# Score stacks gathered by sixteen rows a DMA, eight apart, from terms laid out pair by pair in DRAM

## The chip, the cores and the metric

The kernel runs on one core of a Trainium2 chip. The metric is the device time of one execution in microseconds (us). The core has a matrix engine (TensorE, PE in the rows), a vector engine (VectorE, DVE), a scalar engine (ScalarE, ACT), GpSimd (POOL), and a sync engine (SyncE, SP), and 16 DMA engines that move data between DRAM and the on-chip memory of 128 partitions. In this kernel SP issues nearly all DMAs; a row of "SPq" is SP issuing them.

## The reference

Four small transformer blocks are applied one after another to an activation of 4 sequences x 512 tokens x 128 features. The first two concern us: block 0 is a cross-attention, block 1 a causal self-attention, a cross-attention and a mixture of experts. All of them have 16 heads of 8 features and take exact fp32 products. Cut to the part that the change touches:

```python
q = (target @ wq).reshape(b, tq, 16, 8)
k = (context @ wk).reshape(b, tk, 16, 8)
v = (context @ wv).reshape(b, tk, 16, 8)
scores = jnp.einsum('bqhd,bkhd->bhqk', q, k) * (1.0 / np.sqrt(8))
...
attn = jax.nn.softmax(scores, axis=-1)
out = jnp.einsum('bhqk,bkhd->bqhd', attn, v).reshape(b, tq, d)
```

The context has 154 tokens; in the causal self-attention keys and queries are the same 512 tokens.

## The kernel before

The work is cut into units, one for each sequence of each stage. Units 0 to 3 are the cross-attention of block 0 (stage L0), 4 to 7 the self-attention (SELF), 8 to 11 the cross-attention of block 1 (CROSS). These 12 "exact" units run from the start to about 590 us. Then come the experts (MOE), two quantised attentions, a feed-forward, a grouped attention and another feed-forward, which the change leaves alone.

**The stacks.** A head has only 8 features, and the score product has to be as exact as fp32. So q and k are each split into three bf16 terms, and eight products of terms are summed (`Q_TERMS`, `K_TERMS`: 0·0, 0·1, 1·0, 0·2, 2·0, 1·1, 1·2, 2·1). The eight products are laid under one another along the contraction: 8 products x 8 features = 64 rows (`STACK`) for one head, and two heads make a pair and fill 128 partitions. There are eight pairs. The stack of queries (`q_stack`) is thus [128 partitions, 8 pairs, 512 tokens] in bf16, 1 MB, the stack of keys is `k_stack` (1 MB, units 4 to 7) or `k_stack_ctx` (8 pairs x 160 columns, 320 KB, cross units). Each has two buffers, for even and odd units. A score matmul (L1106, L1110 in cross units, L1115 in self units) takes the 64 rows of one half as a whole, so the order of the rows within a half does not matter, if it is the same for q and k.

**How a stack is made.** VectorE (L1665 to L1667) leaves the three terms in `parts` with the 128 features on the partitions. They go through DRAM: SP writes each term with one DMA (L818, three for k and three for q), waits until they have landed (`k_out`, `q_out`), and reads them back into the stack. For one unit SP does, in order: write k's terms, write q's terms, read the keys (L800), wait for q's terms, read the queries (L807). Self units' first keys are read ahead of q's writes. In unit 0 ScalarE's queue reads the keys (L1493), and SP reads the queries in two lots: two pairs, then six. Behind the queries of unit 0, unit 5 and unit 9 other loads stand in SP's queue: feed-forward weights (L836), the clearing of `by_expert` (L840), and the experts' weights (L844 to L848).

**What waits for it.** TensorE's order is written out by slots. The parts of unit u+1 are made in the first slots of unit u, and the first scores of unit u+1 are placed three slots ahead of the end of unit u (`AHEAD = 3`). At the first score of a unit TensorE waits for the whole stack of keys and of queries. TensorE's queue is in order, so everything behind that matmul waits as well. VectorE takes the row maxima of each score (L1960), ScalarE the exponentials (L1509), TensorE the transposed scores (L1137, L1149, L1155) and the weighted sums (L1175, L1177).

The lines that do it:

```python
if i == 0:
    pe.wait_ge(k_stacked, 32 * len(K_TERMS) * (u + 1))
    if u:
        pe.wait_ge(q_stacked, 32 * len(Q_TERMS) * (u + 1))
```

Of the kernel before, what the change touches and what calls it, by code (L numbers as in the profile page):

```python
# [6 lines left out]
B, TOKENS, CTX, D = 4, 512, 154, 128  # L7
P = 128
# [40 lines left out]

Q_TERMS = [0, 0, 1, 0, 2, 1, 1, 2]  # L50
K_TERMS = [0, 1, 0, 2, 0, 1, 2, 1]
STACK = len(Q_TERMS) * HD

# [342 lines left out]
def build(nc, io, out):  # L396
# [3 lines left out]
    with ctx:  # L400
# [83 lines left out]
        def place(area, at):  # L484

            def put(shape, dt=fp32):
# [8 lines left out]
                if len(shape) == 2:  # L495
# [86 lines left out]
        up_bank = [score[0][:, 0, :], score[0][:, 1, :], score[1][:, 0, :], score[1][:, 1, :]]  # L582


        scratch = {side: nc.dram_tensor(f"{side}_terms", [2 * HD, 3, PAIRS, TOKENS], bf16)
                   for side in "qk"}

        k_terms_ctx = nc.dram_tensor("k_terms_ctx", [2 * HD, 3, PAIRS, P + 32], bf16)

        by_expert = [nc.dram_tensor(f"by_expert{g}", [EXPERT_BLOCKS * P, D], fp32) for g in range(2)]  # L590
        from_expert = [nc.dram_tensor(f"from_expert{g}", [EXPERT_BLOCKS * P, D], fp32) for g in range(2)]
# [191 lines left out]
        with nc.Block() as block:  # L783

            @block.sync
            def _(sp):
                for u in EXACT_UNITS:
                    width = P + 32 if is_cross(u) else TOKENS
                    keys = (k_stack_ctx if is_cross(u) else k_stack)[:, u % 2, :, :]
                    k_terms_of = (k_terms_ctx if is_cross(u) else scratch["k"]).ap()  # L790

                    def read_keys():
                        sp.wait_ge(k_out, 48 * (u + 1))
                        if u >= 2 and u != SELF * B:

                            sp.wait_ge(scoresT_ready, FIRST_SLOT[u - 1])
                        for s in range(2):
                            for n, term in enumerate(K_TERMS):
                                r = slice(s * STACK + n * HD, s * STACK + (n + 1) * HD)
                                sp.dma_start(keys[r, :, :], k_terms_of[s * HD:(s + 1) * HD, term, :, :])\  # L800
                                    .then_inc(k_stacked, 16)

                    def read_queries(pairs, stacked):
                        for s in range(2):
                            for n, term in enumerate(Q_TERMS):
                                r = slice(s * STACK + n * HD, s * STACK + (n + 1) * HD)
                                sp.dma_start(q_stack[r, u % 2, pairs, :], scratch["q"].ap()[s * HD:(s + 1) * HD, term, pairs, :])\  # L807
                                    .then_inc(stacked, 16)

                    for side in "kq":  # L810
                        wide, terms_of = (width, k_terms_of) if side == "k" else (TOKENS, scratch["q"].ap())
                        terms, done, stacked = (K_TERMS, k_out, k_stacked) if side == "k" else (Q_TERMS, q_out, q_stacked)
                        sp.wait_ge(parts_ready, 2 * u + (1 if side == "k" else 2))
                        if u:
                            sp.wait_ge(stacked, 16 * 2 * len(terms) * u)

                        for t in range(3):
                            sp.dma_start(terms_of[:, t, :, :].rearrange("r c k -> c r k"), parts[side][:, t, 0:wide])\  # L818
                                .then_inc(done, 16)
                        if u == SELF * B and side == "k":  # L820

                            read_keys()
                    if u and u != SELF * B:
                        read_keys()
                    sp.wait_ge(q_out, 48 * (u + 1))
                    if u >= 2:

                        sp.wait_ge(scoresT_ready, FIRST_SLOT[u - 1])
                    if u == 0:

                        read_queries(slice(0, 2), q_first)
                    read_queries(slice(0 if u else 2, PAIRS), q_stacked)
                    if u == 0:
                        for dst, src in [(e_b2[:, :], io["L1_xattn_e_b2"]), (ff_w1[:, :], io["L2_xattn_ff_w1"]),
                                         (ff_w2[:, :, :], io["L2_xattn_ff_w2"].rearrange("(c p) d -> p c d", p=P))]:
                            sp.dma_start(dst, src).then_inc(ff_in, 16)  # L836
                    if u == 5:

                        for g in range(2):
# [89 lines left out]
            def _(pe):  # L929
# [152 lines left out]
                def scores_exact(u, i):  # L1082

                    c, n = exact_steps(u)[i]
                    at_step = STEP_BASE[u] + i
                    if i == 0:
                        pe.wait_ge(k_stacked, 32 * len(K_TERMS) * (u + 1))
                        if u:
                            pe.wait_ge(q_stacked, 32 * len(Q_TERMS) * (u + 1))
                        else:  # L1090
                            pe.wait_ge(q_first, 32 * len(Q_TERMS))
                        if stage(u) == L0:
                            pe.wait_ge(pad_ready, u + 1)
                        if is_causal(u):
                            pe.wait_ge(masks_ready, 1)
                    if u == 0 and i == PER_GROUP[0]:
                        pe.wait_ge(q_stacked, 32 * len(Q_TERMS))
                    if at_step >= 2:
                        pe.wait_ge(top_ready, at_step - 1)

                    banks = [(half_rows(s), score[at_step % 2][:, s, :]) for s in range(2)]
                    if is_cross(u):
                        for j in range(2):
                            t, of = 2 * n + j, slice(j * CTX, (j + 1) * CTX)
                            for r, bank in banks:
                                ins = nc.tensor.matmul(bank[:, of], q_stack[r, u % 2, c, t * P:(t + 1) * P],  # L1106
                                                       k_stack_ctx[r, u % 2, c, 0:CTX], start=True, stop=(stage(u) != L0))
                            if stage(u) == L0:
                                for r, bank in banks:
# [289 lines left out]
            def _(act):  # L1399
# [87 lines left out]
                for it in BEFORE[0]:  # L1487
                    item(*it)
                act.wait_ge(k_out, 48)
                for s in range(2):  # L1490
                    for n, term in enumerate(K_TERMS):
                        r = slice(s * STACK + n * HD, s * STACK + (n + 1) * HD)
                        act.dma_start(k_stack_ctx[r, 0, :, :], k_terms_ctx.ap()[s * HD:(s + 1) * HD, term, :, :])\  # L1493
                            .then_inc(k_stacked, 16)
                item("tops", 0, 0)
                for w, (u, g, _, pieces) in enumerate(BLOCKS):
                    n = w - FIRST_SLOT[u]
# [626 lines left out]
            def _(pool):  # L2124
# [15 lines left out]
                def item(name, u, n=None):  # L2140
# [30 lines left out]
                        ins.then_inc(pad_ready, 1)  # L2171
                        pool.wait_ge(pad_ready, b + 1)
                    elif name == "kt":
                        pool.wait_ge(k_stacked, 32 * len(K_TERMS) * (u + 1))
                        two = k_stack_ctx[:, u % 2, :, :].rearrange("p (g z) k -> p g z k", z=2)
                        for s in range(2):
                            r = slice(s * STACK, (s + 1) * STACK)
# [188 lines left out]
```

## Time and profile before

| | |
|---|---|
| median of the runs | 1621.03 us (1616.39 to 1622.45, 3 runs) |
| profiled execution | 1629.24 us, span of its instructions 1627.4 us |
| TensorE busy | 1109.7 us, 68% of the span |
| VectorE busy | 1109.3 us, 68% |
| ScalarE busy | 895.0 us, 55% |
| GpSimd busy | 681.6 us, 42% |
| exact units (where the stacks are used) | 0 to about 590 us |
| granted TensorE clock, mean of the span | 0.815 |

A share of busy time is an average over stages with different limits. What the change is worth is read in the first 590 us, from the stretches in which TensorE stands before a unit's first score. Times in rows are from the start of the span.

### The profile page before, as it was taken

The numbers are of one execution on the slowest core, as the hardware profiler recorded it, in microseconds if no ns is written. First come the engines' busy times: TensorE is split into PE (matmuls) and PEld (weight loads), VectorE is DVE, ScalarE is ACT, GpSimd is POOL, SyncE is SP. The second block draws the span as 40 slices with busy tenths as digits, with TensorE's granted clock in tenths as the row PEclk, the third lists the DMA queues.
The fourth block names the chain that finished last, engine by engine and source line by source line (L and its number), as shares of the span: only waits on it lengthen the run. The fifth ranks groups of instructions, "written<-read, shape, count | busy, mean of one in ns | idle before, by whom it ended". The sixth has DMA issues, their size and how long they took to land.

```text
span 1627.4 us, 28786 instructions
## 1 busy us (share of the span) xinstructions
PE 1109.7 (68%) x9344; PEld 600.2 (37%) x9344; DVE 1109.3 (68%) x3126; ACT 895.0 (55%) x2546; POOL 681.6 (42%) x1054
## 2 busy tenths in 40 slices
PE   2688888787777679784435354444439787898888
PEld 1333344444322238681111121122215544453545
DVE  2577777777666666277989899877765556666533
ACT  1344455545543346347767688888872344545542
POOL 3321010111011323456888888877771245354420
PEclk9899999999998999796555555555559889999999
DMA  6223242022172111217546566655650112111000
GB/s 175 62 47 72 49 120 92 10 72 48 32 150 42 35 41 52 74 40 182 116 95 111 97 110 118 120 109 107 106 106 1 26 40 53 33 28 46 3 1 26
DMA packets 263829, 115.86 MB, mean 71 GB/s; under 512 B 216056, under 2 KB 252544, under 8 KB 261504
## 3 DMA queue, kind: packets, MB, share of 16 engines
q1 hardware_dynamic: 258720, 107.61, 31.6%
q0 software_dynamic: 2048, 4.20, 0.9%
q10 hardware_dynamic: 2912, 2.22, 0.5%
q8 instruction: 75, 1.23, 0.3%
q14 instruction: 74, 0.61, 0.1%
HBM read 38.80 MB, written 16.45 MB: 34 GB/s over the span
## 4 chain that ended last, share of the span: by engine, by line
PE 35%; POOL 19%; issue 17%; DVE 15%; ACT 10%; DMA 2%; SPq 1%; POOLq 0%; another core or an unknown queue 0%; ACTq 0%; DVEq 0%
POOL arena L2268 10%; ACT arena L1562 5%; PE acc L1177 3%; PE trans L1149 2%; POOL inv_total L2257 2%; PE misc L999 2%; PE misc L1005 2%; PE trans L1301 2%; ACT arena L1509 2%; POOL arena L2215 2%; PE score L1313 2%; PE score L1315 2%; PE trans L1155 2%; PE acc L1175 1%; DVE arena L1727 1%
## 5 line engine op out<-in xcount | busy, mean ns | idle before, releaser
L2268 POOL TENSOR_SCALAR arena<-arena,inv_total 128x512 f16<-128x512 f32 (+1 forms) x512 | 302.6, 591 | 55.8 <-DVE inv_total L2038 15.4
L1960 DVE TENSOR_REDUCE minus_top<-score 128x4 f32<-128x616 f32 (+4 forms) x256 | 201.4, 803 | 140.9 <-PE score L1110 54.6
L2134 POOL TENSOR_TENSOR rstd<-spread,minus_half 128x4 f32<-128x4 f32 x36 | 37.7, 1048 | 526.1 <-DVE spread L1643 456.9
L1562 ACT ACTIVATE arena<-score,minus_top,exp_scale 128x512 f32<-128x512 f32 (+1 forms) x340 | 210.6, 626 | 18.1 <-POOL arena L2268 8.1
L1509 ACT ACTIVATE arena<-trans 128x512 f32<-128x512 f32 x240 | 134.5, 596 | 113.8 <-PE trans L1155 107.8
L1600 ACT ACTIVATE arena<-arena,minus_top 128x154 f32<-128x154 f32 x256 | 105.1, 412 | 133.0 <-DVE minus_top L2103 132.9
L1258 PE MATMUL score<-arena 32*128 32x512 bf16 (+1 forms) x340 | 69.0, 458 | 144.1 <-ACT arena L1562 143.2
L2044 DVE TENSOR_REDUCE top_score<-score 128x2 f32<-128x1024 f32 (+1 forms) x128 | 135.7, 1061 | 0.6 <-PE score L1258 0.5
L2288 POOL TENSOR_TENSOR arena<-arena,inv_total 128x512 f32<-128x512 f32 x64 | 66.7, 1041 | 147.4 <-DVE inv_total L2111 133.6
L1562 ACT ACTIVATE arena<-trans,minus_top,exp_scale 128x154 f32<-128x154 f32 (+1 forms) x172 | 105.6, 621 | 16.2 <-POOL arena L2268 11.8
L2098 DVE CUSTOM_DVE_ANT_0 arena<-score,arena 128x154 f32<-128x154 f32 x256 | 66.0, 314 | 62.8 <-PE score L1338 62.4
L2027 DVE TENSOR_SCALAR arena<-arena 128x1024 bf16<-128x1024 f16 x192 | 102.7, 535 | 5.5 <-DMA arena<-arena 5.5
L1553 ACT ACTIVATE minus_top<-top_score,exp_scale 128x2 f32<-128x2 f32 (+1 forms) x192 | 56.5, 294 | 61.4 <-DVE top_score L2044 61.1
L1258 PEld LDWEIGHTS score<-arena 32*128 32x128 bf16 x340 | 14.3, 102 | 195.4 <-ACT arena L1562 178.0
L1177 PE MATMUL acc<-arena 128*32 128x512 f32 (+3 forms) x768 | 80.6, 507 | 4.7 <-issue 4.0
L1258 PE MATMUL trans<-arena 32*128 32x154 bf16 (+1 forms) x172 | 34.7, 451 | 72.0 <-ACT arena L1562 71.8
L1106 PE MATMUL score<-arena 64*128 64x154 bf16 x512 | 45.7, 248 | 54.0 <-issue 32.7
L1527 ACT ACTIVATE arena<-score,arena 128x128 f32<-128x128 f32 x184 | 52.0, 372 | 50.4 <-PE score L1214 43.4
L1277 PE MATMUL acc<-arena 128*32 128x128 bf16 x1536 | 59.2, 307 | 27.8 <-DVE oT L2052 15.2
L1509 ACT ACTIVATE arena<-trans,arena 128x512 f32<-128x512 f32 x80 | 52.3, 687 | 30.6 <-PE trans L1155 27.0
L2044 DVE TENSOR_REDUCE top_score<-trans 128x2 f32<-128x1024 f32 (+1 forms) x64 | 67.4, 1053 | 0.0
L1447 ACT COPY arena<-misc 128x512 bf16<-128x512 bf16 x48 | 28.1, 586 | 70.1 <-PE misc L989 67.3
(282 smaller groups left out, 2902.6 us busy)
## 6 DMA issues: line engine op xcount, KB each, us to landing
arena<-q_terms SPq DMA_DIRECT2D x176, 64.0 KB
late<-arena SPq DMA_DIRECT2D x128, 64.0 KB, 2.0
q_terms<-arena SPq DMA_DIRECT2D x36, 128.0 KB
late<-k_terms SPq DMA_DIRECT2D x64, 64.0 KB
arena<-arena SPq DMA_TRANSPOSE x192, 3.1
by_expert<-zeros SPq DMA_DIRECT2D x2, 1472.0 KB, 17.6
arena<-by_expert SPq DMA_DIRECT2D x10, 256.0 KB, 3.0
from_expert<-arena SPq DMA_DIRECT2D x10, 256.0 KB
```

Source lines behind the costliest of these rows:

```text
L1177: ins = nc.tensor.matmul(acc[32 * j:32 * j + 32, q0:TOKENS], v_cols[:, k, 4 * g + j, :], src, start=(b % half == 0 and k == 0), stop=(last ...
L1258: ins = nc.tensor.matmul(quant_score[i % 3][:, j, z * n:(z + 1) * n], qT_codes[r:r + 32, u % 2, t * P:(t + 1) * P], k4_codes[r:r + 32, u % ...
L1277: ins = nc.tensor.matmul(acc[32 * j:32 * j + 32, P * t:P * (t + 1)], vals[:, 4 * j + i, :], pT_codes[:, (2 * n + j // 2) % CODE_SLOTS, j % ...
L1509: nc.scalar.activation(expT[w % SLOTS], trans[w % 2][:, :], ACT.Exp, bias=bias)\
L1562: ins = nc.scalar.activation(probs[:, i % 3, j, of], quant_score[i % 3][:, j, of], ACT.Exp, bias=minus_top[:, at_col:at_col + 1], scale=ex ...
L1600: ins = nc.scalar.activation(gq_exp_p[:, i % 3, h, :], shifted[:, i % 3, h, :], ACT.Exp, bias=minus_top[:, at_col:at_col + 1], accum_out=t ...
L1960: nc.vector.tensor_reduce(dst, src, axis=AX.X, op=ALU.max, negate=True).then_inc(top_ready, 1)
L2027: nc.vector.tensor_scalar(pT_codes[:, of, :, :].rearrange("p k q -> p (k q)"), pT_raised[:, of, :, :].rearrange("p k q -> p (k q)"), -HALF ...
L2044: nc.vector.tensor_reduce(of_step(top_score, i), src, axis=AX.X, op=ALU.max, negate=True).then_inc(quant_top, 1)
L2098: ins = nc.vector.tensor_tensor_reduce(out=shifted[:, i % 3, h, :], in0=score[i % 2][:, odd, z * CTX:(z + 1) * CTX], in1=mask_add[:, b % 2 ...
L2268: ins = nc.gpsimd.tensor_scalar(codes[:, (i - 1) % CODE_SOURCES, j, to], probs[:, (i - 1) % 3, j, of], inv_total[:, at_col:at_col + 1], HA ...
L2288: nc.gpsimd.tensor_tensor(gq_p[:, v % 2, :, :], gq_exp_p[:, v % 3, :, 0:P], inv.to_broadcast([P, 4, P]), ALU.mult)
```

## The change

In DRAM, a term was stored feature row by feature row: [16 rows, 3 terms, 8 pairs, tokens]. Now it is [3 terms, 8 pairs, 16 rows, tokens]. In the stack, the eight rows of one product used to stand together (rows 0-7 of a half are product 0, 8-15 product 1, and so on, in each half). Now row 8·r + n holds feature r of product n, so one product takes the 16 partitions n, n+8, ..., n+120, in both halves at once.

A write of a term is then one contiguous piece in DRAM, and its access pattern is 128 rows instead of 8 x 16. A read brings one product for both heads of all pairs: 16 partitions, each with 8 runs of one pair (1 KB for 512 tokens, 320 bytes for the 160 columns of a context), where it used to be 8 partitions with one run of 8 KB (or 2560 bytes). A stack takes 8 DMAs in place of 16, with the same bytes. The counts that the waits name are halved accordingly.

```diff
-        scratch = {side: nc.dram_tensor(f"{side}_terms", [2 * HD, 3, PAIRS, TOKENS], bf16)
+        scratch = {side: nc.dram_tensor(f"{side}_terms", [3, PAIRS, 2 * HD, TOKENS], bf16)
...
-        k_terms_ctx = nc.dram_tensor("k_terms_ctx", [2 * HD, 3, PAIRS, P + 32], bf16)
+        k_terms_ctx = nc.dram_tensor("k_terms_ctx", [3, PAIRS, 2 * HD, P + 32], bf16)
...
-                        for s in range(2):
-                            for n, term in enumerate(K_TERMS):
-                                r = slice(s * STACK + n * HD, s * STACK + (n + 1) * HD)
-                                sp.dma_start(keys[r, :, :], k_terms_of[s * HD:(s + 1) * HD, term, :, :])\
-                                    .then_inc(k_stacked, 16)
+                        for n, term in enumerate(K_TERMS):
+                            sp.dma_start(keys[n::PRODUCTS, :, :], k_terms_of[term].rearrange("c r k -> r c k"))\
+                                .then_inc(k_stacked, 16)
...
-                        for s in range(2):
-                            for n, term in enumerate(Q_TERMS):
-                                r = slice(s * STACK + n * HD, s * STACK + (n + 1) * HD)
-                                sp.dma_start(q_stack[r, u % 2, pairs, :], scratch["q"].ap()[s * HD:(s + 1) * HD, term, pairs, :])\
-                                    .then_inc(stacked, 16)
+                        for n, term in enumerate(Q_TERMS):
+                            sp.dma_start(q_stack[n::PRODUCTS, u % 2, pairs, :], scratch["q"].ap()[term, pairs].rearrange("c r k -> r c k"))\
+                                .then_inc(stacked, 16)
...
-                            sp.dma_start(terms_of[:, t, :, :].rearrange("r c k -> c r k"), parts[side][:, t, 0:wide])\
+                            sp.dma_start(terms_of[t].rearrange("c r k -> (c r) k"), parts[side][:, t, 0:wide])\
                                 .then_inc(done, 16)
...
-                for s in range(2):
-                    for n, term in enumerate(K_TERMS):
-                        r = slice(s * STACK + n * HD, s * STACK + (n + 1) * HD)
-                        act.dma_start(k_stack_ctx[r, 0, :, :], k_terms_ctx.ap()[s * HD:(s + 1) * HD, term, :, :])\
-                            .then_inc(k_stacked, 16)
+                for n, term in enumerate(K_TERMS):
+                    act.dma_start(k_stack_ctx[n::PRODUCTS, 0, :, :], k_terms_ctx.ap()[term].rearrange("c r k -> r c k")).then_inc(k_stacked, 16)
```

On SP, for unit 1 (a cross unit), the order is before ("arena" and "late" are the big on-chip buffers in which stacks and parts live, the shape is that of the destination in elements):

```order
L818 DMA k_terms_ctx<-arena 8x16x160 [waits k_stacked,parts_ready]
L818 DMA k_terms_ctx<-arena 8x16x160 x2
L818 DMA q_terms<-arena 8x16x512 [waits q_stacked,parts_ready]
L818 DMA q_terms<-arena 8x16x512 x2
L800 DMA arena<-k_terms_ctx 8x1280 [waits k_out]
L800 DMA arena<-k_terms_ctx 8x1280 x15
L807 DMA arena<-q_terms 8x4096 [waits q_out]
L807 DMA arena<-q_terms 8x4096 x15
```

and with the change, at the same place:

```order
L815 DMA k_terms_ctx<-arena 128x160 [waits k_stacked,parts_ready]
L815 DMA k_terms_ctx<-arena 128x160 x2
L815 DMA q_terms<-arena 128x512 [waits q_stacked,parts_ready]
L815 DMA q_terms<-arena 128x512 x2
L799 DMA arena<-k_terms_ctx 16x8x160 [waits k_out]
L799 DMA arena<-k_terms_ctx 16x8x160 x7
L804 DMA arena<-q_terms 16x8x512 [waits q_out]
L804 DMA arena<-q_terms 16x8x512 x7
```

The order of the steps and the waits are the same; only the number and the form of the DMAs differ. For unit 0 on SP, before:

```order
L818 DMA k_terms_ctx<-arena 8x16x160 [waits parts_ready]
L818 DMA k_terms_ctx<-arena 8x16x160 x2
L818 DMA q_terms<-arena 8x16x512 [waits parts_ready]
L818 DMA q_terms<-arena 8x16x512 x2
L807 DMA arena<-q_terms 8x1024 [waits q_out]
L807 DMA arena<-q_terms 8x1024 x15
L807 DMA arena<-q_terms 8x3072 x16
```

and with the change:

```order
L815 DMA k_terms_ctx<-arena 128x160 [waits parts_ready]
L815 DMA k_terms_ctx<-arena 128x160 x2
L815 DMA q_terms<-arena 128x512 [waits parts_ready]
L815 DMA q_terms<-arena 128x512 x2
L804 DMA arena<-q_terms 16x2x512 [waits q_out]
L804 DMA arena<-q_terms 16x2x512 x7
L804 DMA arena<-q_terms 16x6x512 x8
```

Here too the two lots of queries are halved in number, and nothing moves past anything else.

## Rows read from the trace of the kernel before

**Rows 1.** The page: TensorE's busy time, and the chain that ended last.

```profile
PE 1109.7 (68%) x9344; PEld 600.2 (37%) x9344; DVE 1109.3 (68%) x3126; ACT 895.0 (55%) x2546; POOL 681.6 (42%) x1054
...
PE 35%; POOL 19%; issue 17%; DVE 15%; ACT 10%; DMA 2%; SPq 1%; POOLq 0%; another core or an unknown queue 0%; ACTq 0%; DVEq 0%
```

**Rows 2.** Timeline of PE, matmuls at a stack's wait: start, us, what [idle before].

```profile
32.68 0.31 PE L1106 MATMUL score<-arena 64*128 64x154 bf16 x2 [15.35 <-DMA arena<-q_terms]
43.21 0.31 PE L1106 MATMUL score<-arena 64*128 64x154 bf16 x2 [3.29 <-DMA arena<-q_terms]
75.05 0.31 PE L1106 MATMUL score<-arena 64*128 64x154 bf16 x2 [6.41 <-issue]
114.20 0.31 PE L1106 MATMUL score<-arena 64*128 64x154 bf16 x2 [3.91 <-issue]
154.85 0.31 PE L1106 MATMUL score<-arena 64*128 64x154 bf16 x2 [3.68 <-issue]
191.28 0.61 PE L1115 MATMUL score<-late,arena 64*128 64x512 bf16 x2 [2.89 <-issue]
460.50 0.44 PE L1106 MATMUL score<-arena 64*128 64x154 bf16 x4 [7.31 <-issue]
499.73 0.44 PE L1106 MATMUL score<-arena 64*128 64x154 bf16 x4 [6.70 <-issue]
542.37 0.31 PE L1106 MATMUL score<-arena 64*128 64x154 bf16 x4 [4.65 <-issue]
```

**Rows 3.** The chain that ended last, in order of time: start, us, what.

```profile
21.89 3.82 DMA q_terms<-arena
...
36.33 6.83 DMA arena<-q_terms
...
110.29 3.91 issue
```

**Rows 4.** Timeline of SP's queue, units 0, 1 and 3: start, us, DMAs issued.

```profile
20.66 1.79 SPq L818 DMA_DIRECT2D q_terms<-arena  x3
25.72 10.90 SPq L807 DMA_DIRECT2D arena<-q_terms  x32
...
56.55 1.80 SPq L818 DMA_DIRECT2D q_terms<-arena  x3
...
64.72 7.07 SPq L807 DMA_DIRECT2D arena<-q_terms  x16
...
91.14 1.80 SPq L818 DMA_DIRECT2D q_terms<-arena  x3
93.05 5.49 SPq L800 DMA_DIRECT2D arena<-k_terms_ctx  x16
98.64 5.36 SPq L807 DMA_DIRECT2D arena<-q_terms  x16
```

**Rows 5.** Windows: busy per engine, PEclk, DMA engines' share, GB/s.

```profile
101.00:112.00 11.00, 8.34 (x60) 3.74 (x58) 9.37 (x25) 4.65 (x9) 2.28 (x2) 1.00 0.52 77
112.00:114.00 2.00, 0.00 (x0) 0.00 (x0) 0.24 (x1) 0.00 (x0) 1.60 (x2) 0.62 0.06 8
...
129.30:131.30 2.00, 2.00 (x10) 0.82 (x10) 1.89 (x5) 1.03 (x3) 0.00 (x0) 1.00 0.26 61
...
132.70:135.70 3.00, 3.00 (x19) 1.33 (x19) 1.55 (x2) 1.27 (x2) 0.00 (x0) 1.00 0.48 151
```

**Rows 6.** Line L857 (loads of 256 KB, 128 partitions x 4 runs): issue ns, landing.

```profile
L857 SPq DMA_DIRECT2D arena<-by_expert x12: 359/360/497, 588.2 to 697.6; - x12
...
DMA to landing us min/median/max: 2.9/3.0/3.8
```

**Rows 7.** Windows' sum over seven half-clock stretches behind waits; chain rows, either clock.

```profile
sum 32.95, PE 32.05 PEld 15.97 DVE 15.59 ACT 11.97 POOL 11.21; mean PE 4.58 PEld 2.28 DVE 2.23 ACT 1.71 POOL 1.60
...
115.43 0.85 PE trans L1137 x2
...
509.24 0.61 PE trans L1137 x2
```

More of the change, by code:

```diff
@@ L51 @@
 K_TERMS = [0, 1, 0, 2, 0, 1, 2, 1]
-STACK = len(Q_TERMS) * HD
+PRODUCTS = len(Q_TERMS)
+STACK = PRODUCTS * HD
 STAGES = 9
@@ L796, in read_keys @@
                             sp.wait_ge(scoresT_ready, FIRST_SLOT[u - 1])
-                        for s in range(2):
-                            for n, term in enumerate(K_TERMS):
-                                r = slice(s * STACK + n * HD, s * STACK + (n + 1) * HD)
-                                sp.dma_start(keys[r, :, :], k_terms_of[s * HD:(s + 1) * HD, term, :, :])\
-                                    .then_inc(k_stacked, 16)
-                    def read_queries(pairs, stacked):
-                        for s in range(2):
-                            for n, term in enumerate(Q_TERMS):
-                                r = slice(s * STACK + n * HD, s * STACK + (n + 1) * HD)
-                                sp.dma_start(q_stack[r, u % 2, pairs, :], scratch["q"].ap()[s * HD:(s + 1) * HD, term, pairs, :])\
-                                    .then_inc(stacked, 16)
+                        for n, term in enumerate(K_TERMS):
+                            sp.dma_start(keys[n::PRODUCTS, :, :], k_terms_of[term].rearrange("c r k -> r c k"))\
+                                .then_inc(k_stacked, 16)
+                    def read_queries(pairs, stacked):
+                        for n, term in enumerate(Q_TERMS):
+                            sp.dma_start(q_stack[n::PRODUCTS, u % 2, pairs, :], scratch["q"].ap()[term, pairs].rearrange("c r k -> r c k"))\
+                                .then_inc(stacked, 16)
                     for side in "kq":
                         wide, terms_of = (width, k_terms_of) if side == "k" else (TOKENS, scratch["q"].ap())
-                        terms, done, stacked = (K_TERMS, k_out, k_stacked) if side == "k" else (Q_TERMS, q_out, q_stacked)
+                        done, stacked = (k_out, k_stacked) if side == "k" else (q_out, q_stacked)
                         sp.wait_ge(parts_ready, 2 * u + (1 if side == "k" else 2))
                         if u:
-                            sp.wait_ge(stacked, 16 * 2 * len(terms) * u)
+                            sp.wait_ge(stacked, 16 * PRODUCTS * u)
                         for t in range(3):
-                            sp.dma_start(terms_of[:, t, :, :].rearrange("r c k -> c r k"), parts[side][:, t, 0:wide])\
+                            sp.dma_start(terms_of[t].rearrange("c r k -> (c r) k"), parts[side][:, t, 0:wide])\
                                 .then_inc(done, 16)
@@ L1086, in scores_exact @@
                     if i == 0:
-                        pe.wait_ge(k_stacked, 32 * len(K_TERMS) * (u + 1))
+                        pe.wait_ge(k_stacked, 16 * PRODUCTS * (u + 1))
                         if u:
-                            pe.wait_ge(q_stacked, 32 * len(Q_TERMS) * (u + 1))
+                            pe.wait_ge(q_stacked, 16 * PRODUCTS * (u + 1))
                         else:
-                            pe.wait_ge(q_first, 32 * len(Q_TERMS))
+                            pe.wait_ge(q_first, 16 * PRODUCTS)
                         if stage(u) == L0:
@@ L1096, in scores_exact @@
                     if u == 0 and i == PER_GROUP[0]:
-                        pe.wait_ge(q_stacked, 32 * len(Q_TERMS))
+                        pe.wait_ge(q_stacked, 16 * PRODUCTS)
                     if at_step >= 2:
@@ L2173, in item @@
                     elif name == "kt":
-                        pool.wait_ge(k_stacked, 32 * len(K_TERMS) * (u + 1))
+                        pool.wait_ge(k_stacked, 16 * PRODUCTS * (u + 1))
                         two = k_stack_ctx[:, u % 2, :, :].rearrange("p (g z) k -> p g z k", z=2)
```

## The prediction

> **What bounds the kernel now.** I read the page first. TensorE and VectorE are each busy for two thirds of the span, and of the chain that ended last 17% is "issue" [rows 1]: time in which the engine waited for something that the profile doesn't name. So no engine is full, and the question is where such waits stand. In the timeline of TensorE I then looked for the first score of each unit, since there TensorE waits for the stacks. The reader is to see nine idle stretches in front of exactly these matmuls [rows 2]: 15.35 and 3.29 us in unit 0, then 6.41, 3.91, 3.68 and 2.89 us ahead of units 1 to 4, and 7.31, 6.70 and 4.65 us ahead of units 9 to 11. Units 5 to 8 have none. The chain shows that they aren't slack: the wait ahead of unit 3 is on it, and in unit 0 it runs through the DMAs themselves [rows 3].
>
> That "issue" is the stack comes from the DMA side. For unit 3, SP wrote q's terms from 91.14 us, issued the keys from 93.05 and the queries from 98.64 to 104.0 [rows 4]. But the DMA engines go on until about 112.8: from 101 to 112 us they move 77 GB/s, then they fall silent, and TensorE starts 1.4 us later, at 114.20 [rows 2, 5]. TensorE had come there at 114.20 - 3.91 = 110.29. So the read of 1 MB of queries, some 13 us at 77 GB/s, sets these waits, and not its issue of 5.4 us. Its share of the DMA engines is 0.52, which is 8 of 16, and each of these moves 9.6 GB/s; the write of q's terms in 1 KB pieces, also at 0.48, makes 151 GB/s, 19.7 GB/s for each engine [rows 5]. So the reads use half of the engines, and those at half pace.
>
> **The change, part by part.** *Engines.* Reads went to 8 rows each and writes to an outer dimension of 8, and both ran at about half of the engines' share [rows 5]. Now the outer dimension is 16 for reads and 128 for writes. I expect all 16 engines. The Trainium skill (DMA: Bandwidth & Descriptors, Why a DMA increments its semaphore by 16 and not by 1) says that a DMA is spread over the largest number up to 16 that divides the slowest dimension of both sides; by that rule the trace's 8 becomes 16.
>
> *Pace of one engine.* The trace has no read of 16 rows eight apart. Bounds: 9.6 GB/s (the old reads) and 19.7 GB/s (the writes of 1 KB) for each engine. The pieces are now those of the write, and neighbours in the stack no longer come to the same DMA, so I take the second: 16 x 19.7 = 315 GB/s, 3.3 us for 1 MB, against 6.8 us at the lower bound.
> The Trainium skill (SBUF — State Buffer, Door 1: The DMA port swizzle) gives eight adjacent partitions 2 of 16 ports of some 27 GB/s, thus 54 GB/s. The trace shows 77, so that figure is too low here. By the page, 16 partitions eight apart reach 8 ports, 218 GB/s and 4.8 us for 1 MB; the sum would be the same, with 1.5 us less to spare in each unit.
>
> *Issue.* An old read costs 5.36/16 = 0.34 us of SP's time, an old write 0.60 us [rows 4]; a load over all partitions with 512 runs costs 0.36 us [rows 6]. So runs don't cost SP time by their number. I take 0.40 us for a read with 128 runs, and 0.45 us for a write, with 0.61 us (the write, and its gap) as upper bound. Eight reads: 3.2 us in place of 5.4.
>
> *Landing.* 256 KB over 16 engines land 3.0 us after issue [rows 6]; I take 2.6 us for the last 128 KB of a stack.
>
> *Unit 3 added up.* q's terms ready at 91.14; three writes 1.35; keys 3.2; queries 3.2; landing 2.6: the stack is there at 101.5, 8.8 us before TensorE comes for it at 110.29. With both upper bounds (0.61 us for each issue, 6.8 us for the data, of which about 4 lie behind the last issue) it is 91.14 + 1.8 + 4.9 + 4.9 + 4 = 106.7, still in time. Units 2, 4 and 9 to 11 are alike. Unit 1 is tight: terms ready at 56.55, TensorE there at 75.05 - 6.41 = 68.64. The same sum gives 66.9; with the upper bounds 72.2, and 3.5 us of its wait remain.
>
> So I strike the seven waits of units 1 to 4 and 9 to 11: 6.41 + 3.91 + 3.68 + 2.89 + 7.31 + 6.70 + 4.65 = **35.5 us**.
>
> *Unit 0.* Written from 20.66, landed at 25.72 [rows 3, 4]. On 16 engines the three writes land at about 24.4. Then eight issues of the first lot, 3.2, and 1.5 for its landing (32.68 less the end of the old first lot's issue, 25.72 + 5.45): first scores at 29.1 in place of 32.68, **3.6 us**. TensorE would then be at the second wait at 43.21 - 3.29 - 3.6 = 36.3; that lot is issued by 30.8 and landed by 34, so its **3.3 us** go too. At the upper bounds (no gain in the write, 0.61 us an issue) unit 0 gives about 2 us in all.
>
> *Not all of it arrives.* Behind a struck wait, VectorE's maxima or ScalarE's exponentials can be what is late next; VectorE is busy for 9.37 of the 11 us ahead of unit 3's wait [rows 5]. I take off a tenth of 35.5 + 3.6 + 3.3 = 42.4: 38 us.
>
> *The clock.* Behind each of the seven waits the granted clock is 0.5, the lower level of 1.2 GHz, for 3.4 to 6.5 us, where TensorE had stood still just before; in these 32.95 us TensorE is busy for 32.05 [rows 7]. The same pair of matmuls takes 0.85 us there and 0.61 at full clock [rows 7], so by this pair the work would take 9 us less at full clock; twice the clock could give 16 at most, a wait that stays cold nothing. VectorE has 15.6 us of work in it, so not all of it will be felt; I take **6 us**.
>
> *Costs nothing.* Interleaving the stack's rows: a score matmul takes a half's 64 rows whole. Self units 5 to 7: their stacks already come in time. The later stages have no stack. If the weights behind unit 9's queries start earlier, their room is that which the queries leave; their cover is all of units 9 to 11.
>
> Sum: 38 + 6 = **44 us**. The profiled execution took 1629.2, which gives 1585; it stood 8.2 us above the median of the runs, 1621.0, so I predict **1577 us**.
>
> **The rivals.** *A. The stacks come sooner, but not soon enough* (pace of 9.6 GB/s per engine and issue at 0.61, or a spread over 8 engines only). For: no row shows such a read. Against: unit 3 still had 3 us to spare at the upper bounds. Unit 1 keeps 3.5, unit 0 keeps 5, and at yet slower pace others keep a third: 20 to 30 us are gained, 1591 to 1601.
>
> *B. Another wait takes the place.* TensorE comes to the unit's start sooner and the row maxima aren't done: VectorE is at 85% there [rows 5]. Against: units 9 to 11 go through the same code in about 32 us apart from their wait (499.73 - 460.50 - 6.70), units 2 and 3 in 35 to 37. If half of each wait returned in VectorE and the clock gave nothing: 21 us, 1600.
>
> *C. Slower.* The cost of short runs: a unit's two stacks are now 2048 pieces in place of 256, 128 for each of 16 engines. From 94.5 us, when the keys begin to move, to 112.8, when the stack is full today, is 18.3 us, so the point from which unit 3 is slower than before is 18.3/128 = 143 ns a piece. 1 KB at 19.7 GB/s is 52 ns; at 9.6 GB/s it is 107. If a piece took 200 ns, each of seven units would lose 7 us, some 50 us in all: 1671. For: writes of k's terms, in 320-byte pieces, show only 61 GB/s at a share of 0.26 [rows 5]; but that is 320 bytes in 22 ns of an engine.
> The Trainium skill (DMA: Bandwidth & Descriptors, Specifications) asks for at least 512 bytes, below which a read-modify-write is due; the keys of cross units fall from 2560 to 320. It would make this rival's case, and the row of 22 ns speaks against it.
>
> *D. Nothing changes*: the waits were for something else that stands beside the stack, such as the pad rows that TensorE also waits for in units 0 to 3. Against: units 9 to 11 have no pad rows and the longest waits. Then 1621.
>
> **How the numbers follow.** Forecast 0.70, A 0.14, B 0.08, C 0.04, D 0.04. The forecast's own range is 1562 (all of the 42.4 us of waits and 16 of clock) to 1591 (30 us, without the clock and with 2 in unit 0). The range over all reaches through A and to B: 1562 to 1601. What a measurement tells from no change is 0.5%, 8 us: faster 0.92, same 0.04, slower 0.04.
>
> **What would show it.** In the profile of the changed kernel: the reads at a DMA share near 1 and over 250 GB/s; SP's eight reads in some 3.2 us; no idle stretch over 1 us ahead of the first scores of units 2 to 4 and 9 to 11; the granted clock at 1.00 there; the first score at about 29 us; the experts' start some 44 us earlier. It would be wrong if the reads stayed near half of the engines, if an issue took over 1 us, or if the idle time stood as before in front of a row maximum.

## The result, and the profile after

The changed kernel takes 1577.01 us, the median of 4 runs (1573.29 to 1578.91). The kernel before, run beside it, took 1618.71 (4 runs, 1611.79 to 1622.45). The ratio is 0.9734 with a 95% interval of 0.9696 to 0.9771: 2.7% faster, where 1577 us were predicted. The profiled execution took 1576.97 us, with a span of 1575.2.

The page after, engines and chain:

```profile
PE 1089.3 (69%) x9344; PEld 591.6 (38%) x9344; DVE 1108.5 (70%) x3126; ACT 895.4 (57%) x2546; POOL 679.8 (43%) x1054
...
PE 34%; POOL 21%; DVE 18%; issue 15%; ACT 9%; DMA 2%; SPq 0%; POOLq 0%; ACTq 0%; DVEq 0%
```

Against [rows 1] the reader is to see three things. The engines do the same number of instructions. TensorE is busy for 20.4 us less with the same matmuls, 13.2 of them ahead of the experts' start, where the mean granted clock rose from 0.94 to 0.97. The other 7.3 us lie behind it, where nothing was changed, and are absent in a second profile of the changed kernel (667.1 us busy there before, 659.8 after, 668.0 in the second). And of the chain, "issue" fell from 17 to 15% while VectorE rose from 15 to 18%.

The timeline of TensorE after, first scores of units 0, 1, 2, 3 and 11 (start, us, what, idle before):

```profile
32.52 0.31 PE L1103 MATMUL score<-arena 64*128 64x154 bf16 x2 [14.82 <-DMA arena<-q_terms]
...
67.25 0.24 PE L1103 MATMUL score<-arena 64*128 64x154 bf16 x2 [0.81 <-issue]
...
101.19 0.23 PE L1103 MATMUL score<-arena 64*128 64x154 bf16 x2
...
137.31 0.23 PE L1103 MATMUL score<-arena 64*128 64x154 bf16 x2
...
499.62 0.30 PE L1103 MATMUL score<-arena 64*128 64x154 bf16 x4
```

The eight waits from the second of unit 0 to that of unit 11 [rows 2] are gone, but for 0.81 us in unit 1. The matmuls of units 1 to 3 take 0.23 to 0.24 us where they took 0.31, and the granted clock is 1.00 in the first microseconds of units 1 to 4 and 9 to 11: TensorE no longer comes out of a standstill there. The wait of unit 0 stands nearly as it was.

One other wait has grown. Behind unit 4's first score TensorE now stands still for 1.44 and 0.73 us until VectorE has the row maxima; the longest such wait there was 0.68 us before:

```profile
172.66 0.34 PE L1112 MATMUL score<-late,arena 64*128 64x384 bf16 x2 [1.44 <-DVE minus_top L1954]
```

One label of mine was wrong. The stack that is read from 91 to 104 us before the change, and the score at 114.20, belong to unit 2, and not to unit 3 as the prediction and the heading of [rows 4] have it. The numbers of those sums are not touched. Below it is unit 2.

The timeline of SP's queue after, units 0 and 2 (start, us, DMAs issued):

```profile
21.84 1.55 SPq L815 DMA_DIRECT2D q_terms<-arena  x3
25.72 10.21 SPq L804 DMA_DIRECT2D arena<-q_terms  x16
...
82.20 1.29 SPq L815 DMA_DIRECT2D q_terms<-arena  x3
83.60 5.39 SPq L799 DMA_DIRECT2D arena<-k_terms_ctx  x8
89.10 5.04 SPq L804 DMA_DIRECT2D arena<-q_terms  x8
```

And two windows: the queries' read of unit 2, and the first 5 us of its scores (busy time per engine, the clock granted to TensorE, the DMA engines' share, GB/s):

```profile
91.00:95.00 4.00, 4.00 (x31) 1.78 (x31) 4.00 (x6) 1.86 (x5) 0.00 (x0) 1.00 0.62 199
101.20:106.30 5.10, 4.25 (x57) 2.21 (x53) 5.04 (x11) 4.53 (x8) 3.58 (x4) 1.00 0.00 0
```

A write now costs 1.29/3 = 0.43 us of SP's time, and a read 5.04/8 = 0.63, where it was 0.34 [rows 4]. The eight reads thus take nearly as long to issue as the sixteen did (5.36 us), but behind the last of them hardly anything is left to move: all is issued by 94.14 us, the DMA engines fall silent at about 96, and TensorE comes for it at 101.19. Before, 77 GB/s flowed for 9 us longer than SP issued [rows 4, 5]. Now 199 GB/s flow at a share of 0.62, and it is the issue that holds them back: 128 KB each 0.63 us is 208 GB/s. (The share adds up the time of packets, the pieces that one DMA engine moves at a time; it passes 1 where packets overlap, 1.14 from 432 to 439 us after, so it isn't a strict count of engines. The packets themselves agree with it here: of those that carry data at most 10 were under way at once in the old read, and 8 most of the time; in the new one up to 19. These are counted from the packets' records in the traces.) In the second window TensorE has the full clock, and VectorE is busy for 5.04 of 5.10 us: it is what sets the pace now.

**Where the time came from.** The experts' first sum, a matmul with `ident`, marks the end of all twelve units. The group of these matmuls after (count, ns min/median/max, first and last start):

```profile
L1201 PE MATMUL acc<-ident,arena x46: 272/273/477, 552.2 to 672.4; 128*128 128x128 f32 x46
```

In the kernel before the same group starts at 597.1, so the units gave 44.9 us. The waits struck are 3.29 + 35.5 - 0.8 = 38.0, unit 0's first score gave 0.2, and 6.7 us are the rest, which is what the clock gave, less what was lost elsewhere. (Something was: from unit 0's first score to that of unit 1, without the waits for stacks, it is 75.05 - 32.68 - 6.41 - 3.29 = 32.7 us before, and 67.25 - 32.52 - 0.81 = 33.9 after, with TensorE busy for 25.9 and 27.0 us of it.) In a second profile of the changed kernel the experts start at 554.6, so that the gain is 42.5 to 44.9 us. From there on no DMA was changed, yet this part differs between executions: 1030.3 us before, 1023.0 after, 1028.2 in a second profile of the changed kernel. That is why the two spans lie 52.2 us apart. The medians lie 41.7 apart. The experts' start is the better measure of the change, and I use it beside the ratios below.

### The profile page after: what moved, and what is told of

Read it like the earlier page. It is cut to its first block, busy times and chain, and to the rows that moved or that the text cites. A ratio compares the mean times of both kernels' runs of the same rounds, so it can differ in the third digit from the quotient of the medians.

```text
span 1575.2 us, 28586 instructions
## 1 busy us (share of the span) xinstructions
PE 1089.3 (69%) x9344; PEld 591.6 (38%) x9344; DVE 1108.5 (70%) x3126; ACT 895.4 (57%) x2546; POOL 679.8 (43%) x1054
## 4 chain that ended last, share of the span: by engine, by line
PE 34%; POOL 21%; DVE 18%; issue 15%; ACT 9%; DMA 2%; SPq 0%; POOLq 0%; ACTq 0%; DVEq 0%
POOL arena L2262 12%; ACT arena L1556 4%; PE acc L1174 3%; DVE minus_top L1954 2%; POOL inv_total L2251 2%; PE trans L1146 2%; PE misc L996 2%; PE misc L1002 2%; PE trans L1298 2%; ACT arena L1503 2%; PE score L1310 2%; PE score L1312 2%; DVE arena L1721 2%; PE trans L1152 1%; DVE top_score L2038 1%
## 5 line engine op out<-in xcount | busy, mean ns | idle before, releaser
L1521 ACT ACTIVATE arena<-score,arena 128x128 f32<-128x128 f32 x184 | 52.4, 370 | 41.7 <-PE score L1211 41.6
L1556 ACT ACTIVATION_READ_ACCUMULATOR arena<-score,minus_top,exp_scale 128x1 f32 x340 | 66.7, 196 | 0.0
L1152 PE MATMUL trans<-arena 64*128 64x512 bf16 (+3 forms) x384 | 63.9, 329 | 0.0
```

The lines of the kernel that those rows point to most:

```text
L1152: ins = nc.tensor.matmul(to, ones[r, j, :], top_rows[r, g % 2, q0:TOKENS], start=False, stop=True)
L1556: ins = nc.scalar.activation(probs[:, i % 3, j, of], quant_score[i % 3][:, j, of], ACT.Exp, bias=minus_top[:, at_col:at_col + 1], scale=ex ...
```

## The experiments

The theory: the gain is that of the struck stack waits and the clock behind them, and the stacks come sooner because a read goes to 16 partitions that lie eight apart. The rivals: what helps is (R1) the layout in DRAM, with writes in one piece and runs of 1 KB; (R2) the order of the rows alone; (R3) the waits are of little worth, and the time comes from elsewhere. Medians are set against the kernel before in the same series: 1628.36 us (29 runs) for the first four, 1626.67 (11 runs) for the others. The ratios are estimates of their own and not quotients of these medians; the two differ by 0.2% at most, which matters in experiment 4 alone.

### 1. The layout and the writes alone

The kernel before, with the terms in DRAM pair by pair and written in one piece; the rows of a stack, and so the sixteen reads to eight adjacent partitions, stay as they were.

```
-  scratch ... [2 * HD, 3, PAIRS, TOKENS]
+  scratch ... [3, PAIRS, 2 * HD, TOKENS]
...
-  sp.dma_start(terms_of[:, t, :, :].rearrange("r c k -> c r k"), parts[side][:, t, 0:wide])
+  sp.dma_start(terms_of[t].rearrange("c r k -> (c r) k"), parts[side][:, t, 0:wide])
...
-  sp.dma_start(keys[r, :, :], k_terms_of[s * HD:(s + 1) * HD, term, :, :])
+  sp.dma_start(keys[r, :, :], k_terms_of[term, :, s * HD:(s + 1) * HD, :].rearrange("c r k -> r c k"))
...
```

> New layout in DRAM and writes in one piece, but the stack's rows as before: 16 reads a stack, each 8 adjacent partitions with 8 runs of 1 KB. Theory (number of engines and neighbouring rows set the pace): reads stay on 8 engines at 80 GB/s or less, the waits ahead of units 1 to 4 and 9 to 11 stay; if an issue with several runs costs 0.6 us, 16 of them take 10 us and the stacks come later still. 1610 to 1650 us. Rival (the layout in DRAM does it): as the changed kernel, 1575 to 1585 us.

1625.03 us (10 runs), ratio 0.9972 [0.994, 1.0003]. The queries' read of unit 2 in the windows, and below it the waits of units 1 and 2 in the timeline of TensorE:

```profile
103.00:116.00 13.00, 9.54 (x72) 4.30 (x67) 11.18 (x28) 6.25 (x11) 2.35 (x3) 1.00 0.59 77
```

```profile
77.60 0.31 PE L1106 MATMUL score<-arena 64*128 64x154 bf16 x2 [10.50 <-issue]
...
117.78 0.31 PE L1106 MATMUL score<-arena 64*128 64x154 bf16 x2 [3.88 <-issue]
```

The 77 GB/s of [rows 5] are unchanged, and the waits are still there: 10.50, 3.88, 2.12 and 2.91 us ahead of units 1 to 4, 6.72, 6.90 and 7.10 ahead of units 9 to 11, 40.1 us in all where it was 35.5. Most of the difference is in unit 1. That isn't put down to the layout: in experiment 4, whose DMAs are those of before, the first score of unit 1 is as late (78.46). R1 falls: the layout by itself brings nothing that this measurement can tell. The issue is unchanged too, 5.51/16 = 0.34 us a read, though each has eight times the runs.

### 2. Sixteen rows eight apart, without the new layout

The changed kernel with the old layout in DRAM and the old writes. A read still goes to 16 partitions eight apart, but each row comes in one run (8 KB for queries).

```
...
-  sp.dma_start(q_stack[n::PRODUCTS, u % 2, pairs, :], scratch["q"].ap()[term, pairs].rearrange("c r k -> r c k"))
+  sp.dma_start(q_stack[n::PRODUCTS, u % 2, pairs, :], scratch["q"].ap()[:, term, pairs, :])
...
```

> Rows eight apart and 16 a DMA as in the changed kernel, but the layout in DRAM as before: one run of 8 KB (2560 bytes) a row, writes to an outer dimension of 8. Theory: 16 engines, and without several runs an issue costs 0.3 to 0.4 us in place of 0.63; the stack is there 4 to 5 us sooner, which no unit waits for but unit 0: 1572 to 1578 us, first score at about 30 us in place of 32.5. Rival (runs of 1 KB or the one-piece write matter): some of the waits return, 1585 us or more.

1590.37 us (4 runs), ratio 0.9774 [0.9725, 0.9822]. By its time it fell in the rival's range (1585 and more), but the changed kernel stood in another series, so I ran it once more beside a repeat of the changed kernel:

> The changed kernel once more, on the same chip as the other three, so that they can be set against it: ratio to the kernel before 0.970 to 0.977.

> Long runs (layout in DRAM as before, writes to an outer dimension of 8, rows eight apart, 16 a read) beside the changed kernel on one chip. Theory (the gain is all in the 16 rows eight apart, the layout and the one-piece writes have cover): equal to the changed kernel within 0.3%. Rival (the runs or the writes earn something): 4 to 8 us slower than it.

The changed kernel: 1587.32 us (6 runs), ratio 0.9754 [0.9715, 0.9793]. The one with the old layout: 1585.23 (6 runs), 0.9755 [0.9714, 0.9797]. They are equal within what can be told, which is about 6 us: of the rival's 4 to 8 us the times alone exclude only the upper part. The experts start at 556.8 and 552.6 here, and at 552.2 and 554.6 in the changed kernel. The queries' read of unit 2 in the first of the two runs, in SP's timeline and below it in a window:

```profile
89.95 4.95 SPq L804 DMA_DIRECT2D arena<-q_terms  x8
```

```profile
92.00:96.00 4.00, 3.83 (x29) 1.51 (x26) 4.00 (x7) 1.86 (x4) 0.00 (x0) 1.00 0.72 211
```

So the gain, as far as it can be told, is in the 16 rows eight apart, and pieces of 1 KB (320 bytes for a cross unit's keys) show neither help nor harm. I had expected a read of 16 runs to be issued in 0.3 to 0.4 us. That missed: it takes 4.95/8 = 0.62, as with 128 runs. The cost must come from something else, which the next kernel shows.

### 3. The rows eight apart, but eight rows a read

The kernel before with one thing changed, in three places: where a product's rows stand.

```
-  r = slice(s * STACK + n * HD, s * STACK + (n + 1) * HD)
+  r = slice(s * STACK + n, (s + 1) * STACK, len(Q_TERMS))
```

> Kernel before with one edit: the stack's rows eight apart, still 16 reads of 8 rows and 8 KB runs, old layout in DRAM. Still 8 engines. Theory (half of the old slowness is that neighbouring partitions of one DMA share a way into the memory): a read packet takes 420 to 550 ns in place of 820, queries come at 130 GB/s or more, stack of unit 2 at about 107 us, before TensorE comes; nearly the whole gain, 1577 to 1590 us. Rival (only the number of engines counts): 77 GB/s and 1615 to 1622 us.

1632.49 us (10 runs), ratio 1.0033 [1.0, 1.0066]. The expectation of the time was wrong: no gain, and it lies in neither range. SP's timeline in unit 2, and below it a window in the queries' read:

```profile
105.26 9.39 SPq L800 DMA_DIRECT2D arena<-k_terms_ctx  x16
114.75 9.33 SPq L807 DMA_DIRECT2D arena<-q_terms  x16
```

```profile
117.00:125.00 8.00, 4.78 (x34) 2.20 (x34) 5.83 (x20) 3.25 (x6) 2.74 (x3) 1.00 0.39 118
```

What I had expected of the data did come: 118 GB/s at a share of 0.39 is 18.9 GB/s for each engine in use, where the adjacent rows have 9.3 (77 at 0.52). A packet of 8 KB took 427 ns in the mean, and 865 before. But a read now costs SP 9.33/16 = 0.58 us in place of 0.34, the same for keys of 20 KB and queries of 64 KB, and sixteen of them take 9.3 us. The data of 1 MB took about 13 us before; now issue takes most of that, and the keys ahead of it take 9.4 in place of 5.5. The last read is issued at 124.08, and the first score of unit 2 follows at 126.10, 2.0 us later, where it was 10.2 before: it is the issue that now sets the wait. The waits stay (11.63, 3.59 and 3.17 us ahead of units 1 to 3, none over 1 us ahead of unit 4, 6.06, 6.41 and 6.08 ahead of units 9 to 11), and unit 0 starts at 38.05, 5.4 us later. So R2 falls as well. What a read costs to issue goes by whether its partitions are adjacent: 0.34 us if so, 0.58 to 0.63 if they are eight apart, whether it has 8 or 16 rows, one run a row or eight. Rows apart make an engine move twice as much, but without sixteen rows a read, which halve the number of the dearer issues, they bring nothing.

The other half wasn't tried: sixteen rows a read in two blocks of eight adjacent partitions, the stack's old order, so that the engines double but not their pace. An estimate from the numbers above is 16 x 9.3 = 149 GB/s, 7 us for a stack of queries, which would still be ahead of TensorE in unit 2. So that the rows have to stand apart for the gain is not shown.

### 4. The waits filled with work

The kernel before, whose TensorE multiplies `ident_bf` uselessly ahead of each of the seven waits, about as long as the wait lasts. It waits as before, but doesn't stand still.

```
+  FILL = {1: 26, 2: 15, 3: 14, 4: 10, 9: 31, 10: 28, 11: 19}
...
+  if u in FILL:
+      pe.wait_ge(top_ready, at_step - 1)
+      for _ in range(FILL[u]):
+          nc.tensor.matmul(score[at_step % 2][:, 0, :], ident_bf[:, :], ..., start=True, stop=True)
```

> Kernel before, with matmuls of no use in front of the seven waits (26, 15, 14, 10, 31, 28, 19 of 512 columns, into a score bank that the next score overwrites), so that TensorE stays busy while it waits. They leave nothing out. The waits for the stacks stay. Theory (the changed kernel's gain is the waits, and some 6 us of clock behind them): the granted clock stays at 1.00 behind the waits and the time falls by 4 to 8 us, 1611 to 1615 us. Rival (VectorE or ScalarE hide the slow stretches, the clock gives nothing): no change, 1617 to 1620 us.

1619.49 us (12 runs), ratio 0.9966 [0.9937, 0.9995], some 5.5 us with an interval from 0.8 to 10.3; the medians lie 8.9 us apart. Unit 2 in TensorE's timeline, then in a window, and last the group of the experts' first sums:

```profile
113.70 3.41 PE L1091 MATMUL score<-ident_bf 128*128 128x512 bf16 x15
117.31 0.24 PE L1112 MATMUL score<-arena 64*128 64x154 bf16 x2 [0.20 <-issue]
```

```profile
117.30:122.40 5.10, 5.09 (x57) 2.53 (x57) 3.99 (x8) 3.21 (x5) 4.37 (x11) 1.00 0.01 3
```

```profile
L1210 PE MATMUL acc<-ident,arena x46: 272/273/476, 591.8 to 711.8; 128*128 128x128 f32 x46
```

The stack comes no sooner, but the granted clock is 1.00 behind it, where it was 0.5 [rows 7], and so in the other filled waits but that of unit 1, where 3.8 us stayed empty and the clock behind them was 0.64. The experts start at 591.8 in place of 597.1: 5.3 us for the clock. That is one pair of executions, and two of the same kernel differ by 2.4 us here in the changed kernel and by 4.2 in that of experiment 2. So the size is rough; that the clock gives something is shown by the times too. It is in keeping with the 6.7 us that the struck waits leave over.

### 5. The waits put back

The changed kernel, but from unit 1 on SP first reads the queries into a buffer that nobody uses, and then into the stack: the same DMAs once more, and so 5 us of SP's time and 1 MB.

```
...
+  for n, term in enumerate(Q_TERMS):
+      sp.dma_start(spare[n::PRODUCTS, :, :], scratch["q"].ap()[term, pairs].rearrange("c r k -> r c k"))\
+          .then_inc(spared, 16)
...
```

> The changed kernel, but from unit 1 on SP reads the queries into a spare buffer first, so that each stack is full some 5.1 us later. Nothing is left out. Theory (a unit starts at the later of TensorE's coming and the stack's landing; the changed kernel has 0 us to spare in unit 1 and some 4 to 8 in the others): a wait of 5 to 6 us ahead of unit 1, 0 to 2 us each ahead of units 2 to 4, 9 to 11; 8 to 14 us slower than the changed kernel. Rival (the waits were not the stacks'): no change beyond 1 us, or a like delay of 5 us in all units, 35 us and more.

1595.54 us (6 runs), ratio 0.9821 [0.9783, 0.9859]: 8.2 us above the repeat of the changed kernel by the medians, and the experts start at 567.9 in place of 554.6, 13.3 us later (the stretch behind them was 4.8 us shorter in this execution than in the other, with no change in it). The waits of units 1 and 10 in TensorE's timeline, and below them that of unit 1 in the repeat of the changed kernel:

```profile
71.66 0.31 PE L1111 MATMUL score<-arena 64*128 64x154 bf16 x2 [6.09 <-issue]
...
474.01 0.31 PE L1111 MATMUL score<-arena 64*128 64x154 bf16 x4 [3.28 <-issue]
```

```profile
66.61 0.24 PE L1103 MATMUL score<-arena 64*128 64x154 bf16 x2 [2.22 <-issue]
```

Made later, the stacks bring part of the waits back: 6.09, 0.71, 2.36, 3.28 and 2.20 us ahead of units 1, 2, 9, 10 and 11, which is 14.6 us in all and 12.4 more than in the repeat. The time comes back with them. R3 falls: the gain is in these waits. Units 9 to 11 have 2.2 to 3.3 us of wait here, more than the 0 to 2 that I had expected, where 5 us were added: their stacks have some 2 to 3 us to spare in the changed kernel, not more.

### 6. Unit 0's first lot by two queues

What is left of the stack waits is nearly all in unit 0. In the changed kernel the first lot's products 4 to 7 are issued by ScalarE's queue:

```
-  read_queries(slice(0, 2), q_first)
+  read_queries(slice(0, 2), q_first, 4)
...
+  act.wait_ge(q_out, 48)
+  for n in range(4, PRODUCTS):
+      act.dma_start(q_stack[n::PRODUCTS, 0, 0:2, :],
+                    scratch["q"].ap()[Q_TERMS[n], 0:2].rearrange("c r k -> r c k")).then_inc(q_first, 16)
```

> The changed kernel, but four of the eight reads of unit 0's first lot of queries go over ScalarE's queue. Theory (SP's 0.63 us an issue set unit 0's first score): the first lot is issued in 2.5 us in place of 5.1, first score at about 30 us in place of 32.5, 2 to 3 us faster than the changed kernel. Rival (data or landing set it): no change.

1581.03 us (6 runs), ratio 0.9725 [0.9686, 0.9765]. The timelines of the queues and of TensorE, unit 0:

```profile
20.75 1.29 SPq L815 DMA_DIRECT2D q_terms<-arena  x3
24.15 7.68 SPq L804 DMA_DIRECT2D arena<-q_terms  x12
...
24.47 2.54 ACTq L1491 DMA_DIRECT2D arena<-q_terms  x4
...
28.59 0.31 PE L1103 MATMUL score<-arena 64*128 64x154 bf16 x2 [11.17 <-DMA arena<-q_terms]
```

From the first read's issue to the first score it is 28.59 - 24.15 = 4.4 us, and 32.52 - 25.72 = 6.8 in the changed kernel: 2.4 us less. The other 1.6 us of the 3.9 lie ahead of the reads, for the greater part in VectorE's work before the write, which no edit touches (see unit 0's first wait, below). The experts start at 549.4, against 552.2 and 554.6. It has the lowest ratio of all, 6 us under the repeat of the changed kernel by the medians, but the two intervals overlap by more than half, so the trace shows this gain and the times don't. Part of it, as said, isn't the edit's.

## Why the prediction was right

- **What bounds, and the waits to strike: right.** 38.0 of 38.8 us went. The two forecasts that hang on it held: no wait over 1 us ahead of units 2 to 4 and 9 to 11, and unit 1 tight, with 0.8 us left in one execution and 2.2 in the other, where the upper bounds gave 3.5. In the other execution the clock behind that wait was 0.66. The time to spare was taken too high: 8.8 us were predicted for unit 2, and some 5 are there (the DMA engines fall silent at 96, TensorE comes at 101.19); units 9 to 11, which were called alike, have 2 to 3.
- **16 engines: right.** The share reaches 0.62 to 0.72 with reads that are issued slower than they move, and the old layout with the same 16 rows shows it too. The share alone would be a weak sign, as it was 0.59 in experiment 1 with eight rows a read, but up to 19 data packets were under way at once, and 16 in experiment 2, where the old reads had at most 10 before and 12 in experiment 1.
- **Pace of one engine, 19.7 GB/s: right**, and by one of its two stated reasons: 199 GB/s at 0.62 is 20.1 for an engine, and 18.9 where only the rows were put apart. Neighbouring partitions in one read halve it. The other reason, pieces of 1 KB like the write's, has little part in it: with pieces of 8 KB it was 18.3 (211 at 0.72), and with 1 KB to adjacent rows 8.2 (77 at 0.59).
- **Issue of a read, 0.40 us: mis-sized.** It measured 0.63, just above the upper bound of 0.61. I had read from [rows 6], whose load goes over adjacent partitions, that runs cost nothing, and that is so; that a step between partitions costs 0.25 to 0.3 us, no row of before showed. It cost the kernel nothing in units 2 to 11, as the sum held near the upper bounds too. A write, taken at 0.45, measured 0.43.
- **A share near 1 and over 250 GB/s: wrong**, for the same reason. The reads are bound by issue at about 200 GB/s.
- **Unit 0's first wait, 3.6 us: wrong, it gave 0.2.** Two terms failed. Eight issues and the landing behind them took 5.1 + 1.7 = 6.8 us, not 4.7. And the reads began at 25.72 as before, not at 24.4: q's terms did land sooner after the write's issue (25.72 - 21.84 = 3.9 us in place of 5.1), but the write was issued 1.2 us later, mostly as a VectorE operation ahead of it, whose code the change doesn't touch, took 1.63 us and not 0.83. In the kernel with two queues, where it took 0.82 and the write went out at 20.75, the reads began at 24.15. So the write's part was right and was lost to that operation; the issue's part was an error.
- **A tenth off for VectorE's sake: it came out by luck.** It offset the error of unit 0: 38 us were predicted for all waits, and 38.2 were struck. That isn't what the tenth stood for. VectorE did become what sets the pace at a unit's start, as rival B has it. In the first 9 us of unit 4 TensorE waits 2.9 us for row maxima, where it was 1.5 before; the sum over all units wasn't taken. The chain after, ahead of unit 2's first score at 101.19, runs through it (start, us, what):

```profile
99.48 0.81 DVE minus_top L1954
```

- **The clock, 6 us: right in kind, and in size as far as can be told**, with 5.3 by filling the waits (an interval from 0.8 to 10.3 by the runs), and 6.7 as what is left over, less what was lost elsewhere.
- **Rivals.** A (too slow) holds for unit 1 alone, in small. B took 1.4 us in unit 4, as above; what it took in all is open. C (the cost of short pieces) did not show itself: with pieces eight times as long nothing changed. In the Trainium skill (DMA: Bandwidth & Descriptors, Specifications) the full rate asks for transfers of at least 512 bytes. The trace agrees as to the rate: the 320-byte pieces of the keys move at 62 GB/s and a share of 0.31, 12.5 for an engine, where the 1 KB pieces have 20.1. It doesn't show in the times, where issue is what binds. D falls with experiment 5.
- **The sum of 44 us**: 44.9 and 42.5 by the experts' start in the two profiles, 41.7 by the medians of the first comparison, 39.4 in the second series. That the median came within 0.1 us of 1577 is luck: the medians of one kernel differ by 10 us between the series.

## What to carry to other kernels

A read that is slow at half of the engines has two causes that can be told apart in the windows: GB/s divided by (share x 16) says how fast an engine goes, the share roughly how many go (packets that overlap make it too high); here rows eight apart doubled the first, and sixteen rows a read raised the second. Which of the two would have been enough alone is shown for one only: rows apart were not. But count the issues too: a DMA to partitions with a step costs the queue nearly twice, so that putting the rows apart without halving the number of reads gained nothing. And in this kernel the layout in DRAM and the length of runs, from 1 KB to 8 KB, were worth nothing that the runs could tell.

## What the hardware showed unexpectedly

- SP's time for one DMA, in the stretches of unit 2 (some others are longer, as 7.07/16 = 0.44 us in [rows 4]): 0.34 us to 8 adjacent partitions with 1 run or 8 runs a row; 0.58 us to 8 partitions eight apart; 0.62 and 0.63 us to 16 partitions eight apart with 1 and 8 runs a row. Bytes (20 KB or 64 KB) made no difference.
- A write from 128 partitions costs 0.43 us in one piece, and 0.60 us with an outer dimension of 8 (1.29 and 1.80 us for three).
- ScalarE's queue issues the same reads at the same price, 2.54/4 = 0.64 us, and two queues issue side by side.
- Reads to eight adjacent partitions get 9.3 GB/s for each engine, to eight partitions eight apart 18.9.
- A VectorE operation of unit 0 takes 0.82 or 1.63 us, according to whether it or a GpSimd operation on other data starts first. The timelines of the two engines in the kernel with two queues, and below it in the changed kernel:

```profile
19.90 0.82 DVE L1665 TENSOR_TENSOR arena<-arena 128x512 bf16<-128x512 f32 x1
...
20.25 1.59 POOL L2136 TENSOR_TENSOR x<-x,rows 128x512 f32<-128x512 f32 x1
```

```profile
20.18 1.63 DVE L1661 TENSOR_TENSOR arena<-arena 128x512 bf16<-128x512 f32 x1
...
19.94 1.32 POOL L2132 TENSOR_TENSOR x<-x,rows 128x512 f32<-128x512 f32 x1
```

  In all ten profiles, that of before among them, it is so: five times VectorE starts first and takes 0.82 to 0.83, with 1.59 for GpSimd, and five times GpSimd starts first, with 1.63 and 1.32. The second to start pays. Since q's write waits for VectorE, this moves the first stack by 0.8 us. What decides who starts first wasn't tried. It may not be chance alone: GpSimd starts first in four of the five profiles with the new layout in DRAM, and in one of the five with the old.
- Waits of TensorE of 3 to 7 us were followed by 3.4 to 6.5 us at half clock each [rows 7]. Filling six of the seven, and part of the seventh, gave 5.3 us in one pair of executions.
